# Two attention-and-FFN layers on one core: the weight-scale search with every second unit folded, five square buffers, 24 units rounded on ScalarE, products on GpSimd and a written-out order of calls

## The reference, cut to what matters

```python
for s in SHRINKS:                      # 16 values, 0.4 to 1.0
    scale = base * s                   # base = max|w| of the block / 15
    deq = clip(round(wb / scale), -15, 15) * scale
    err = sum((deq - wb) ** 2)         # over the 64 weights of the block
    best_scale = where(err < best_err, scale, best_scale); best_err = minimum(err, best_err)
deq = clip(round(wb / best_scale), -15, 15) * best_scale
h = relu(x @ deq(w_fc).T);  x = x + (h * h) @ deq(w_proj).T
```

## Time and profile before

| what | value |
|---|---|
| time, median of three runs | 416.27 us |
| the profiled execution, its own time | 414.8 us |
| its span, first to last instruction | 413.0 us |
| mean granted TensorE clock | 0.971 of 2.4 GHz |
| busy: PE, DVE, ACT, POOL | 346.8, 341.7, 248.3, 170.5 us |
| the 64 folds on POOL | 89.0 us, 1403 ns each |
| the 64 sums on DVE | 42.8 us, 680 ns each |
| the 64 squares on ACT | 69.5 us |

### The profile page before, as it was taken

How to read it: one execution, slowest core, us unless ns; L and a number is a source line. 1 busy time by engine, 2 the same in 40 slices (tenths; PEclk the granted TensorE clock), 3 DMA queues, 4 the chain that set the end, 5 groups by cost and what they waited for, 6 DMA issues and landing times.

```text
span 413.0 us, 8385 instructions
## 1 busy us (share of the span) xinstructions
PE 346.8 (84%) x3222; PEld 253.1 (61%) x3222; DVE 341.7 (83%) x877; ACT 248.3 (60%) x371; POOL 170.5 (41%) x203
## 2 busy tenths in 40 slices
PE   2876697738857867979997888999999999989996
PEld 1442474413322323656796776887888888778885
DVE  4999879993898597645878899999989999999950
ACT  4799969967778798312645778864676565211000
POOL 3364654456886989812200110526214127621000
PEclk9999999987997999989999999999899999999999
DMA  8920000000000000350000000000000000000000
GB/s 257 362 79 2 2 0 0 2 1 0 2 0 1 0 2 0 97 160 1 2 0 2 1 2 0 3 2 2 2 5 12 14 2 17 2 14 2 17 14 27
DMA packets 11144, 11.42 MB, mean 28 GB/s; under 512 B 608, under 2 KB 10592, under 8 KB 11104
## 3 DMA queue, kind: packets, MB, share of 16 engines
q1 hardware_dynamic: 11104, 10.88, 8.3%
HBM read 9.83 MB, written 1.05 MB: 26 GB/s over the span
## 4 chain that ended last, share of the span: by engine, by line
DVE 43%; PE 26%; POOL 12%; issue 11%; ACT 6%; DMA 1%; POOLq 0%; DVEq 0%; ACTq 0%
POOL arena L343 10%; PE pair L754 9%; PE pair L592 4%; PE pair L718 3%; DVE i L1554 3%; DVE arena L1614 2%; DVE stats L1274 2%; DVE arena L1352 2%; DVE arena L1610 2%; PE pair L740 2%; DVE s L1548 2%; POOL arena L326 2%; DVE XN L1287 2%; PE pair L531 2%; DVE arena L1317 1%
## 5 line engine op out<-in xcount | busy, mean ns | idle before, releaser
L343 POOL TENSOR_TENSOR arena<-arena 128x512 f32<-128x512 f32 x64 | 89.0, 1403 | 59.0 <-ACT arena L1023 23.3
L718 PE MATMUL pair<-arena,EDT 128*128 128x256 f32 x256 | 60.2, 383 | 0.0
L754 PE MATMUL pair<-EU,arena 128*128 128x256 f32 x256 | 58.4, 382 | 0.6 <-DVE arena L1638 0.6
L1352 DVE TENSOR_REDUCE arena<-arena 128x16 f32<-128x512 f32 x64 | 42.8, 680 | 18.4 <-POOL arena L343 18.3
L548 PE MATMUL pair<-arena,WQ 128*128 128x512 fp8e4 x112 | 35.1, 397 | 22.1 <-ACT arena L1020 18.9
L754 PEld LDWEIGHTS pair<-EU,arena 128*128 128x128 f32 x256 | 47.9, 190 | 7.4 <-issue 1.0
L718 PEld LDWEIGHTS pair<-arena,EDT 128*128 128x128 f32 x256 | 47.1, 190 | 6.5 <-ACT arena L1153 0.2
L393 POOL TENSOR_TENSOR arena<-arena 128x512 f32<-128x512 f32 x20 | 27.1, 1370 | 49.4 <-ACT arena L1145 49.4
L1023 ACT ACTIVATE arena<-pair 128x1024 f32<-128x1024 f32 x32 | 33.3, 1041 | 14.7 <-PE pair L560 14.7
L560 PE MATMUL pair<-arena 128*128 128x512 fp8e4 x128 | 40.5, 399 | 0.0
L1020 ACT ACTIVATE arena<-pair,sq_bias 128x1024 f32<-128x1024 f32 x32 | 36.2, 1131 | 4.6 <-PE pair L560 3.7
(11 more groups left out here) (196 smaller groups left out, 667.5 us busy)
## 6 DMA issues: line engine op xcount, KB each, us to landing
arena<-in_L_ffn_e_down_dram SPq DMA_DIRECT2D x1, 2048.0 KB, 12.2
EU<-in_L_ffn_e_up_dram SPq DMA_DIRECT2D x1, 2048.0 KB, 9.2
arena<-in_L_ffn_w_fc_dram SPq DMA_DIRECT2D x2, 512.0 KB, 5.3
X<-in_x_dram SPq DMA_DIRECT2D x1, 1024.0 KB, 5.9
arena<-in_L_ffn_w_proj_dram SPq DMA_DIRECT2D x1, 1024.0 KB, 14.6
GUW<-in_fside_BxS2xS_dram SPq DMA_DIRECT2D x1, 1024.0 KB, 12.1
out_dram<-arena SPq DMA_DIRECT2D x8, 128.0 KB, 1.7
CTX<-in_ctx_dram SPq DMA_DIRECT2D x1, 512.0 KB, 4.9
```

The lines of the kernel that those rows point to most:

```text
L343: pool.tensor_tensor(qf(g), sq[:, :, 0:32], sq[:, :, 32:64], ALU.add).then_inc(s["folded"], 1)
L718: last = pe.matmul(bk2(4 + i % 2)[:, r, :], EDT[:, k, at:at + P], xT4[:, b % 2, k, :], start=(k == 0), stop=(k == 1))
L754: last = pe.matmul(bk2(7)[:, n, :], PR[:, n, e, :], EU[:, e, :], start=(e == 0), stop=(e == EROWS - 1))
L1352: dve.tensor_reduce(err[:, g // NS % 2, :, g % NS], qf(g), AX.X, ALU.add).then_inc(s["reduced"], 1)
```

## The change

It rebuilds the search and leaves everything behind it as it was, but for two `ffn1` calls.

- **Folds.** Only even units are folded (`halved`). For an odd unit DVE sums the 1024 squares themselves, straight out of `qd`.
- **Buffers.** Five square buffers (`QDEPTH`) in place of three.
- **Rounding.** ACT rounds units with g % 8 in 1, 3, 5 (24 of them), DVE the other 40 (before: 32 and 32).
- **Products.** The three products of a chunk (`scale_weights`, `scale_quantised`, `dequantise`) go from DVE to POOL, for chunks 1, 2, 3 the first and for chunks 0, 1, 2 the other two: nine instructions of 1024 columns. `split(0)` stays on DVE.
- **Step matrices** are made in eight pieces between other calls (`step_tables`), and PE waits for the piece it needs.
- **Order.** The loops over g are replaced by a written list of calls on each of the four engines.

```diff
-        W_UNIT = {27: 0, 42: 1, 58: 2}
-        FFN1_UNIT = {29 + 4 * i: i for i in range(HID // P)}
+        def halved(g):
+            return g % 2 == 0
+        def folds(g):
+            return sum(halved(i) for i in range(g + 1))
         def qf(g):
-            return (qf_early if g < QF_LATE else qf_late)[:, g % DEEP]
+            return (qf_early if g < QF_LATE else qf_late)[:, (folds(g) - 1) % DEEP]
+        def qd(g):
+            return (qd_early if g <= QF_LATE else qd_late)[g % QDEPTH]
         def on_act(g):
-            return 0 < g < NU and g % 2 == 1
+            return g > 0 and g % 8 in (1, 3, 5)
...
+            def scale_weights(c):
+                pool.wait_ge(s["prepared"], c + 1)
+                if c >= 2:
+                    pool.wait_ge(s["diff"], NS * (c - 1))
+                pool.tensor_tensor(blocks(qu[:, c % 2, :]), blocks(W[:, c * CH:c * CH + CH]), spread(rbase), ALU.mult
+                                   ).then_inc(s["scaled"], 1)
+            def scale_quantised(c):
+                pool.wait_ge(s["chosen"], c + 1)
+                pool.tensor_tensor(blocks(qt), blocks(W[:, c * CH:c * CH + CH]), spread(rscale), ALU.mult
+                                   ).then_inc(s["qscaled"], 1)
+            def dequantise(c):
+                pool.wait_ge(s["qrounded"], c + 1)
+                pool.tensor_tensor(blocks(W[:, c * CH:c * CH + CH]), blocks(qi), spread(scale), ALU.mult
+                                   ).then_inc(s["wquant"], 1)
...
             def sum_error(g):
-                dve.wait_ge(s["folded"], g + 1)
-                dve.tensor_reduce(err[:, g // NS % 2, :, g % NS], qf(g), AX.X, ALU.add
-                                  ).then_inc(s["reduced"], 1)
+                if halved(g):
+                    dve.wait_ge(s["folded"], folds(g))
+                    squares = qf(g)
+                else:
+                    dve.wait_ge(s["squared"], g + 1)
+                    squares = blocks(qd(g))
+                dve.tensor_reduce(err[:, g // NS % 2, :, g % NS], squares, AX.X, ALU.add).then_inc(s["reduced"], 1)
...
-            for g in range(NU):
-                if g + 4 < NU and not on_act(g + 4):
-                    clip_round(g + 4)
-                if g >= 3:
-                    sum_error(g - 3)
...
+            clip_round(62)
+            sum_error(57)
+            sum_error(58)
+            sum_error(59)
+            clip_round(63)
```

More of the change, by code:

```diff
@@ new lines, in _ @@
+            dequantise(0)
+            fold(34)
+            fold(36)
+            fold(38)
+            scale_quantised(1)
+            fold(40)
+            scale_weights(3)
+            fold(42)
+            square_hidden(0)
+            fold(44)
+            split(3)
+            fold(46)
+            dequantise(1)
+            fold(48)
+            square_hidden(1)
+            fold(50)
+            fold(52)
+            square_hidden(2)
+            scale_quantised(2)
+            fold(54)
@@ L582, in _ @@
[L582 to L585, removed]
+            keys_transposed()
+            attention_inputs(0)
+            unit(0)
+            attention_inputs(1)
+            unit(1)
+            unit(2)
+            energy(0)
+            unit(3)
+            unit(4)
+            energy(1)
+            unit(5)
+            energy(2)
+            unit(6)
+            x_transposed(0)
+            unit(7)
@@ new lines, in _ @@
+            unit(27)
+            x1_transposed(0)
+            unit(28)
+            unit(29)
+            unit(30)
+            unit(31)
+            unit(32)
+            x1_transposed(1)
+            unit(33)
+            x1_transposed(2)
+            unit(34)
+            unit(35)
+            unit(36)
+            w_transposed(0)
+            unit(37)
+            unit(38)
+            x1_transposed(3)
+            unit(39)
+            unit(40)
+            unit(41)
+            ffn1(0)
@@ new lines, in _ @@
+            ffn1(1)
+            unit(42)
+            unit(43)
+            unit(44)
+            unit(45)
+            ffn1(2)
+            unit(46)
+            ffn1(3)
+            unit(47)
+            unit(48)
+            unit(49)
+            unit(50)
+            unit(51)
+            unit(52)
+            w_transposed(1)
+            unit(53)
+            unit(54)
+            ffn1(4)
+            ffn1(5)
+            unit(55)
+            unit(56)
+            unit(57)
+            unit(58)
@@ L587, in ffn2 @@
+            unit(59)
+            unit(60)
+            unit(61)
+            unit(62)
+            w_transposed(2)
+            unit(63)
+            ffn1(6)
+            ffn1(7)
             def ffn2(b, o, tiles=range(TPB)):
@@ L1419, in gate_weight_maxima @@
+            scale_quantised(3)
+            round_quantised(3)
+            dequantise(3)
             def gate_weight_maxima(b):
```

591 lines of the change are left out of this document (450 added, 141 removed).

## The result

The changed kernel takes 394.03 us, median of four runs (392.33 to 395.16), against 416.11 us: a ratio of 0.947, 95% interval 0.943 to 0.952. The prediction was 406.6 us, range 399.5 to 413.5. The direction was right, the size not: 22.1 us instead of 9.7. In a later comparison the same kernel took 395.18 us against 415.13 (run e17, ratio 0.951, 0.946 to 0.956).

A forecast was written before the change was run, and what follows sets the result against it. DVE was taken as the bound of the search: 143.9 us of work and 11.5 idle end the last sum at 159.7. A transpose 8.9 us earlier plus 0.8 for the clock gives 416.3 - 9.7 = 406.6 us, range 399.5 to 413.5.

The forecast's parts named there:

- DVE's work as the frame: In the search, DVE alone was taken as the bound, the other engines having room of some 12% or more.
- the first rival: DVE hardly waits in the search, 3.5 us idle and the relief doubled: 399.6 us, chance 0.13.
- DVE's own work: DVE's work up to the last sum of the search would go from 138.3 to 143.9 us.
- relief: Less company from POOL shortens DVE's instructions in the search: -3.0 us for all, of which 1.9 for clips.
- DVE's idle time: DVE's idle time in the search would fall from 28.6 to 11.5 us, with a third of fold and PE waits kept.
- Five buffers: Five square buffers let sums lag some units behind the squares, so late folds find other work ahead; no separate size.
- The end of the search: From last unit to the transpose of chunk 3: 12.6 us, the transpose at 169.3, a gain there of 8.9 us.
- PE's way: PE's list behind the last unit, five `ffn1` blocks included: 156.7 + 12.6 = 169.3 us, the later way.
- DVE's way: DVE's chain for chunk 3 behind the last sum, 6.95 us long: 159.7 + 6.95 = 166.7 us.
- Behind the search: After the transpose of chunk 3 all shifts with it; half of 1.7 us lost by PE's matmuls, 0.8, comes back.
- Added waits on POOL: Waits of POOL's products for DVE, and of `w_transposed(2)` for `dequantise(2)`, priced at nothing; one product, 2.4 us, if uncovered.
- The slower rival: POOL's nine products each stop a DVE clip or small instruction, at 1.6 us costing 14.4: 421.0 us, chance 0.06.

The follow-up runs named there:

- e17: The changed kernel itself once more, nothing altered, in a later comparison: 395.18 us, ratio 0.951 to the kernel before.
- e5: The changed kernel with the nine products back on DVE, each right behind the call that makes its scale: 403.98 us, ratio 0.971 to the kernel before.
- e6: The changed kernel with eight roundings moved back from DVE to ACT, the old split: 400.35 us, ratio 0.961 to the kernel before.
- e2: The kernel before with the written order alone: all units folded, three square buffers, 32/32 rounding, products on DVE: 415.8 us, ratio 1.005.
- e3: The changed kernel with three square buffers instead of five, nothing else: 419.2 us, ratio 1.014 to the kernel before.
- e10: The changed kernel with four square buffers instead of five: 395.5 us, ratio 0.954 to the kernel before.
- e15: The changed kernel with one block, `ffn1(6)`, moved ahead of `w_transposed(2)` and unit 63: 394.72 us.
- e4: The changed kernel with all 64 units folded on POOL, each odd fold behind the even one: 419.2 us, ratio 1.014 to the kernel before.
- e11: The changed kernel with no fold at all, every sum reading 1024 columns: 402.03 us, ratio 0.968 to the kernel before.
- e1: The changed kernel with the old loops over g as order on all four engines, all other parts new: 401.0 us, ratio 0.969 to the kernel before.

## Why the prediction was wrong, step by step

- **What bounds it, DVE's work as the frame: right.** e5 moved 8 us of work back and 10 us of time came back. That ACT is the near second, as the first rival's "against" said for the last two chunks, fits e6 but is not shown by it alone.
- **DVE's own work, 143.9 us: 2.8 too high.** Measured 141.1. I had added lengths of single instructions to a busy time. In the rows neighbours overlap (a clip of 0.69 us is followed 0.60 us later by the next instruction), and the busy time of a window does not count that twice. The lengths of all DVE instructions up to the last sum add up to 151.8 us before and 156.8 after, +5.0 where my terms give +5.6. But where DVE no longer waits between instructions, more of them overlap, 15.7 us instead of 13.4, and that is 2.3 of the 2.8 us. Term by term in lengths: the sums +16.5 (16.9 predicted), the products -15.7 as priced, the clips +2.9 where I had 7.4 less 1.9, since I priced eight more at the old mean, and all else +1.3 where I had 1.1 of relief. With the old loops DVE's work came out at 144.2, 0.3 from the forecast, with lengths of 159.6 in sum; in the written order they are 2.8 us shorter. That is no rule: in e2 the same kind of order made DVE's work 6.2 us longer.
- **DVE's idle time, 11.5 us: the step that failed most.** Measured 5.1, which is 6.4 of the 9.2 us by which the last sum came early (150.5, not 159.7). I kept a third of each wait, with no row behind the third. In the loops 8.9 us were left, of which 3.3 for folds. In the written order no wait for a fold or for PE's differences is left, and that was the first rival, given 0.13 with 3.5 us of idle time. Its time, 399.6, was too high as well, since I cut it short by 4 us for ACT and PE.
- **Five buffers.** I named the lag that they allow, and did not weigh it. e3 puts a price on it: 25 us, more than the whole change brings. e10 shows that four would have done nearly all.
- **The end of the search: right, with some luck.** 12.6 us from the last unit to the transpose, 12.8 measured, PE's way the later one. DVE's way was 7.6 us and not 6.95. But e15 shows that ACT's relu holds the `ffn1` blocks up nearly as long as PE's queue does, and I had not looked at it.
- **Behind the search.** I took 0.8 us for the clock and the profile has 1.8: the four matmuls alone are 1.6, and one stretch of 20 us with a clock of 0.91 is left instead of two. With the 8.9 too little at the transpose that makes the 9.9 us between 9.7 and the profiled 19.6.
- **Added waits on POOL: right.** No wait of DVE for a product in the trace; `w_transposed(2)` started at once.
- **The slower rival, products that stop DVE.** It did not come at its price: the 4.4 us that came back in e5 are some 0.5 us for each product, under the threshold of 1.1, and its clips are 74 ns shorter. The mechanism is there for folds in number. In e4, 32 more folds raise DVE's work from the 123.8 us that shorter sums would leave (141.1 - 17.3) to 148.8, 0.78 us for each fold. The Trainium skill, SBUF — State Buffer, section "SBUF: two separate sides", has VectorE and GpSimd share a port pair as an exclusive lock, held for the whole instruction. The traces agree in kind: a clip that is 0.63 us at its shortest takes up to 2.39 in e4, and up to 2.06 in e11, without a fold. How much it costs in all is told by the runs alone: some 0.36 us for each of the first 32 folds (0.25 against e10) and 0.78 for each of the second, while a fold saves DVE 0.53. This fits half the folds being near the best: of 0, 32, 40 and 64 folds, the times are 402.0, 394.0, 392.6 and 419.2 us, the last one with DVE's new waits in it.

## What to carry to other kernels

An order and the depth of its buffers are one thing: here the order alone gave nothing, the parts alone 13.6 us, and the same order with three buffers instead of five lost more than everything. When an engine gets more work and a new order at once, do not keep "a third of its waits" by feel: ask for each wait whether the new order puts other ready work ahead of it, and give the case "none is left" its full weight. And when work moves to GpSimd or away from it, price its company on VectorE as well as its own length. Add lengths to lengths and busy time to busy time, since the records of neighbours overlap.

## What the runs showed of the hardware

- With 0, 32 and 64 folds on GpSimd, VectorE's clip of 1024 columns took 749, 816 and 1099 ns in the mean, with a shortest of 629 in each. The same 40 clips beside the same GpSimd work took 816 in one order and 1020 in another.
- A wait of 2.83 us in front of PE's fp32 matmuls was followed by a granted clock of 0.91 over the next 20 us and by four matmuls of 3.48 us, nearly twice 1.88, as at the lower of the two clock levels (1.2 instead of 2.4 GHz); with the wait filled by 20 transposes it was 1.00 and 1.88 us.
- Behind the transpose of chunk 3 the work is the same in all nineteen traces. Cut into stretches of 20 us, PE is busy 215.8 us there where no stretch has a granted clock of 0.91 (e2, e3), 217.1 to 217.5 where one has, and 218.9 to 219.0 where two have (before, e1, e4, e15): some 1.5 us for each.
